# A graph, attention and MLP layer on one core: target rows of the last 18 edge tiles added by their gather

## The reference

```
feat  = concat(xn[src], xn[dst])               # 8192 x 2048
e     = relu(feat @ W + b)                     # three kinds of edge, each with its own W (2048 x 1024)
logit = e @ W_a + b_a                          # one number per edge
alpha = softmax of logit over the edges with the same dst
z     = segment_sum(alpha * xn[src], dst)
new   = relu(concat(xn, z) @ W_node + b_node)
```

## Time and profile before

| engine | busy us | share of the span | instructions |
|---|---|---|---|
| TensorE (PE) | 598.5 | 94% | 2858 |
| VectorE (DVE) | 505.2 | 80% | 843 |
| ScalarE (ACT) | 280.6 | 44% | 467 |
| GpSimd (POOL) | 219.1 | 34% | 177 |

### The profile page before, as it was taken

How to read it: one execution, slowest core, us unless ns; L and a number is a source line. 1 busy time by engine, 2 the same in 40 slices (tenths; PEclk the granted TensorE clock), 3 DMA queues, 4 the chain that set the end, 5 groups by cost and what they waited for, 6 DMA issues and landing times.

```text
span 635.2 us, 8449 instructions
## 1 busy us (share of the span) xinstructions
PE 598.5 (94%) x2858; PEld 465.9 (73%) x2860; DVE 505.2 (80%) x843; ACT 280.6 (44%) x467; POOL 219.1 (34%) x177
## 2 busy tenths in 40 slices
PE   5999999999999999969999999999999989999845
PEld 3788888888888887758888888888886327887422
DVE  6868961659859798968969978899989996648885
ACT  3335324443435253546454445754435994412201
POOL 3000040277636747236627735255110000214320
PEclk9999999999999999979999999999999999999987
DMA  8852563699999999788979959699984213895514
GB/s 326 345 188 97 208 225 124 215 376 415 417 407 356 390 389 398 299 314 299 366 292 319 409 202 382 223 329 325 393 278 181 85 27 135 295 256 188 155 39 127
DMA packets 44910, 171.43 MB, mean 270 GB/s; under 512 B 5572, under 2 KB 5956, under 8 KB 37700
## 3 DMA queue, kind: packets, MB, share of 16 engines
q1 hardware_dynamic: 20016, 86.19, 36.3%
q0 software_dynamic: 21744, 79.90, 35.0%
q10 hardware_dynamic: 3108, 4.81, 2.5%
HBM read 154.08 MB, written 16.80 MB: 269 GB/s over the span
## 4 chain that ended last, share of the span: by engine, by line
PE 56%; DVE 14%; issue 11%; DMA 8%; ACT 7%; POOL 3%; DVEq 0%; another core or an unknown queue 0%; POOLq 0%; ACTq 0%
PE bank_low L1638 15%; PE bank_low L1640 15%; PE bank_low L1639 15%; DMA w_raw<-in_wt 4%; DMA gathered_dst<-edge_tables,dst_row 2%; ACT w_hi L710 2%; ACT hot_hi L834 2%; DVE w_lo L1012 2%; PE bank_high L1640 2%; PE bank_high L1638 1%; PE bank_high L1639 1%; DVE gathered_rows L1191 1%; PE bank_high L1870 1%; PE bank_low L1993 1%; DMA edge_tables<-stage 1%
## 5 line engine op out<-in xcount | busy, mean ns | idle before, releaser
L1638 PE MATMUL bank_low<-w_hi,xT_hi 128*128 128x512 f32 x476 | 188.5, 396 | 6.3 <-ACT bank_low L741 5.4
L1640 PE MATMUL bank_low<-w_hi,xT_lo 128*128 128x512 f32 x476 | 186.1, 391 | 0.0
L1639 PE MATMUL bank_low<-w_lo,xT_hi 128*128 128x512 f32 x476 | 186.0, 391 | 0.0
L623 POOL DMA_INDIRECT gathered_rows<-edge_tables,src_row x68 | 99.2, 1459 | 156.6 <-DVE gathered_rows L1197 112.9
L710 ACT ACTIVATE w_hi<-w_raw 128x2048 fp32r<-128x2048 f32 x49 | 93.9, 1916 | 121.9 <-DMA w_raw<-in_wt 70.5
L1012 DVE TENSOR_TENSOR w_lo<-w_raw,w_hi 128x2048 fp32r<-128x2048 f32 x49 | 112.0, 2290 | 32.9 <-ACT w_hi L710 32.4
L1638 PEld LDWEIGHTS bank_low<-w_hi,xT_hi 128*128 128x128 f32 x476 | 89.9, 189 | 25.6 <-ACT bank_low L741 5.8
L1640 PEld LDWEIGHTS bank_low<-w_hi,xT_lo 128*128 128x128 f32 x476 | 89.8, 189 | 19.1
L1639 PEld LDWEIGHTS bank_low<-w_lo,xT_hi 128*128 128x128 f32 x476 | 90.0, 189 | 18.2
L1191 DVE TENSOR_TENSOR gathered_rows<-gathered_rows,gathered_dst 128x1024 f32<-128x1024 f32 x68 | 82.9, 1219 | 10.3 <-DMA gathered_dst<-edge_tables,dst_row 6.5
L623 POOL DMA_INDIRECT gathered_dst<-edge_tables,dst_row x68 | 80.8, 1189 | 20.7 <-issue 20.7
(11 more groups left out here) (304 smaller groups left out, 882.2 us busy)
## 6 DMA issues: line engine op xcount, KB each, us to landing
w_raw<-in_wt SPq DMA_DIRECT2D x54, 1024.0 KB
edge_tables<-stage SPq DMA_DIRECT2D x32, 256.0 KB
bias_bc<-in_bias_rows ACTq DMA_DIRECT2D x16, 256.0 KB
x_in<-in_x SPq DMA_DIRECT2D x4, 512.0 KB, 9.4
xn_scratch<-xn SPq DMA_DIRECT2D x4, 512.0 KB, 6.5
node_top<-stage SPq DMA_DIRECT2D x8, 256.0 KB
mix_out<-stage SPq DMA_DIRECT2D x8, 256.0 KB
xn_raw<-xn_scratch SPq DMA_DIRECT2D x4, 512.0 KB, 7.9
```

The source lines that it names most:

```text
L623: pool.indirect_dma_start(dest, None, table_d[0:nodes, :], bass.IndirectOffsetOnAxis(ap=index[:, t:t + 1].bitcast(U32), axis=0), compute_o ...
L1638: pe.matmul(dest, lh, rh, start=start and i == 0, stop=False, skip_group_check=True)
L1639: pe.matmul(dest, lh, rl, start=False, stop=False, skip_group_check=True)
L1640: last = pe.matmul(dest, ll, rh, start=False, stop=last_one, skip_group_check=True)
```

## The change

Tiles 50 to 67 leave the list `ADDED_HERE`. So the second branch of GpSimd's loop and of `edge_tile` applies to them. GpSimd's wait before the loads of `dst_bc` is for the 50 adds that VectorE still makes.

```diff
-ADDED_HERE = list(range(T_GATHERED))
+ADDED_HERE = list(range(50))
...
         pool.wait_ge(dst_stored, 16)
-        pool.wait_ge(row_added_here, T_GATHERED)
+        pool.wait_ge(row_added_here, len(ADDED_HERE))
```

## The result

The changed kernel takes 648.55 us (median of 4 runs, 648.01 to 650.67), the kernel before 641.4 us (4 runs, 640.56 to 643.44): 1.0113 times the time, 95% interval 1.008 to 1.0146. It is slower by 7.2 us; the forecast was 7.0 (a median of 648.3).

A forecast was written before the change was run, and what follows sets the result against it. The prediction took TensorE, full from 402 to 465 us, as the bound, with DMA engines 91.7% taken. Shift 7.3 less 0.3 gives 7.0 us: 644.1 profiled, plus 4.2 to the median, 648.3; range 641.2 to 652.

The forecast's parts named there:

- Nothing to gain: Removing 18 VectorE adds, 20.5 us, gives back at most the 0.3 us TensorE wait at 401.9 us.
- The price of an accumulating gather: Each accumulating gather takes 2.74 us of all 16 DMA engines against 1.43 plain, so 1.3 us more for each of 18.
- Place 1: Tiles 50 to 53, before 402 us: loss 0.2, gain 0.3, taken as -0.3 to 0, up to +3 if adds land late.
- Place 2: Tiles 59 to 67, from 404 us: crowded DMA engines land add 64 near 456 us and add 67 at 469 us.
- (a): At PR1's h1, due 457.10 us: late add 64 makes TensorE wait some 2.4 us for `w_lo`.
- (b): At the transposes, line 1788: after add 67 the last minimum ends at 470.95 us, so TensorE waits 3 us more.
- (c): At the lookup, line 1809: `hot_T` comes late, TensorE waits 1.5 us, and the lookup ends at 477.0 us instead of 469.66.
- A: Rival, both places: each add lands before VectorE comes to it, so nothing slows: 641.1 us; chance 0.17, including 0.05 for gain.
- B: Rival, last tiles: accumulating costs no more than plain; the issue chain alone shifts the end 2.9 us: 644.0 us; chance 0.20.
- C: Rival, behind TensorE's new waits: the clock drops too, 2 to 4 us on top: 650.3 to 652.3; chance 0.18 with D.
- D: Rival, tiles 52 and 53: it also breaks at place 1, +1 to +3 us on top of 648.3; chance 0.18 with C.
- The rule of the skill: For gathers at both places: 2.0 us plus bytes over 436 GB/s, 3.2 us, no accumulating surcharge; time would not change.

The follow-up runs named there:

- accumulate_beside: Kernel before with VectorE's adds and order kept; only the target gathers of tiles 50 to 67, into their own buffer, accumulate: 649.71 us, ratio 1.016.
- only_50_58: Kernel before with target rows of tiles 50 to 58 alone added by their gather, 59 to 67 by VectorE: 641.46 us, ratio 1.0011.
- only_65_67: Kernel before with target rows of tiles 65 to 67 alone added by their gather: 646.25 us, ratio 1.0109.
- plain_65_67: Kernel before with tiles 65 to 67 in the new gather order, but plain second gathers overwriting the source rows, sum left out: 641.75 us, ratio 1.0046.
- only_59_67: Kernel before with target rows of tiles 59 to 67 alone added by their gather: 650.18 us, ratio 1.0139.
- plain_second: Changed kernel, same issues, order and waits, but second gathers of tiles 50 to 67 plain, overwriting source rows, sum left out: 641.39 us, ratio 1.0009 to before.
- control: The kernel before, unchanged, run and profiled once more: 642.16 us, ratio 1.0016; profiled execution 641.18 us.
- tiles_26_28: Kernel before with target rows of tiles 26, 27 and 28 alone added by their gather: 645.08 us, ratio 1.0062.
- lag_1: Changed kernel with the target gather issued one turn after the source gather instead of two: 647.0 us, ratio 1.0161 to the kernel before.
- held_65_67: Kernel before with only tiles 65 to 67 added by gather and the three dst_bc loads held back until dot 67: 649.67 us, ratio 1.0168.

## Why the prediction was right

- **Nothing to gain (at most 0.3 us):** right. The wait at 401.9 is gone, and of the 20.5 us saved on VectorE 19.3 come back as waiting at line 1197. That VectorE's adds are worth nothing there follows from the waits of TensorE, not from VectorE's 60.99 of 63 us.
- **The price of an accumulating gather (2.74 us of 16 engines, from the earlier trace rows):** right. accumulate_beside gives 2.83 at the same bytes; in the kernel after q0 takes 64.2% of 404 to 470 us, 42.4 us, for nine plain and eleven accumulating ones: (42.4 - 12.9) / 11 = 2.68. The rows for it came from other tensors, and that didn't matter: the packets took 327 or 328 ns there too.
- **Place 1 (tiles 50 to 53, -0.3 to 0):** right. The adds of tiles 52 and 53 were issued at 374.63 and 378.43; VectorE waited 1.6 and 2.0 us for them, TensorE had no wait at line 1888, and only_50_58 bears out nine tiles in all. The prediction let the landing take 7 us; from issue to dot it was 6.5 and 10.3. In only_50_58 tile 52 waited 3.0 us, and TensorE 0.9 at a `w_lo`: the margin is thin.
- **Place 2, landing of adds 64 and 67 (456 and 469):** the dots started at 455.66 and 469.87, in an execution that was 1.3 us ahead at the first L1888 (378.45 against 379.78), so 1 to 2 us later than forecast when counted from there. The mechanism was right: the landing of add 67 sets everything behind it. The working that gave its time is weaker than the number. It summed all DMA work from 404 us on, 70.4 us, as if every microsecond of it were in the way of add 67. By that sum, half the surcharge should cost about half and three adds (3.9 us more against 4.8 free) nothing. only_65_67 costs 1.09%, 7 us, and 50 to 58 cost nothing that can be told. The pace of the dots explains the second half: a tile needs 1.43 + 2.83 = 4.3 us of the engines, and beside the 47.2% of q1 and q10 that is 8 us of time, about the 7.7 between the dots of tiles 53 and 59, but far more than the 3.3 behind tile 59. The first half, three adds that cost nearly as much as nine, the prediction's working can't give. Free engine time in the stretch as a whole (4.8 us) was the wrong measure; what counts is the slack of the last landing, and plain_65_67 shows that there is none. Its total came out right partly by luck.
- **(a) TensorE waits 2.4 us at `w_lo`:** 2.65 us, but at another place. The waits of ScalarE in the kernel after, from 402 to 472:

```profile
ACT w_hi L710 <- DMA w_raw<-in_wt: 27.8, 4, 11.5
ACT stage L731 <- DMA mix_out<-stage: 7.7, 2, 6.8
```

  A store of the output took so long that ScalarE waited 6.76 us for its buffer, until 451.56, and seeded the next bank with the bias only at 452.25, from where TensorE starts. In only_59_67 it is `w_lo`, 1.3 us. Not only the gathers are late: over the same stretch of before ScalarE waited 17.8 us for weights, and 4.4 at most for such a store. The prediction counted the loads and stores as load on the gathers and did not ask what they do when late.
- **(b) 3 us more at line 1788:** 3.27. The slow clock behind the first wait had taken 1.5 us before; without it the wait would have been some 4.8, so the agreement of the size is partly chance.
- **(c) 1.5 us at line 1809:** there was no wait, but the 1.5 us were there. The transposes and the first matmuls behind them ran at the lower clock (0.54 over 471.90 to 475.10) and took 1.5 us longer, which filled the time in which TensorE would have waited for `hot_T`. VectorE's way from the last minimum to `hot_T`, on which the step rests, took 4.2 us, forecast 4.3.
- **Rivals.** A (hidden) is out by every run with accumulating gathers of tiles 65 to 67. B (chain alone, 644.0) is out by plain_second, 641.39, with a stretch only 0.4 us longer than `control`'s. C was half right: the clock did go, at waits of 2.65 and 3.27 us and not only at one near 5.4, but it put nothing on top, since it filled waits. D did not occur in the kernel after.
- **The sum.** It gave one shift of 7.3 us at the lookup. That shift was 8.6 against `control` and 9.2 against the execution that the sum started from. The profiled execution took 648.01, where the prediction had 644.1; the medians differ by 7.2. So the mechanism held and the size was some 1 to 2 us short; that the medians came within 0.2 us of the forecast is luck.
- **The rule of the skill.** In plain_second and in the kernel after the same bytes go in the same order, and the time differs by 7 us. The fit of the Trainium skill, page "DMA: Bandwidth & Descriptors", section "Anatomy of one DMA — SWDGE (gpsimd) path", gives both kinds of gather the same estimate, 3.2 us, so by it the two kernels would take the same time. The runs do not agree.

**Open.** The 16.7 us of the last add in only_65_67 are accounted for only by the estimate of 4.2 us of engine time at q0's share; how the engines divide their time among the queues wasn't tried. Why the profiled stretch of accumulate_beside holds only 6.0 us of a loss of about 10, and where tiles_26_28 loses 4, isn't shown. That the clock fell because of the waits is read from where it fell; no run removed the waits and kept the rest of the change.

## What to carry to other kernels

Work moved from a compute engine to a DMA is paid in the DMA engines' time: here an accumulating gather cost about twice a plain one of the same bytes, and a price taken from other tensors held within 4%. Before moving such work, look at the DMA share of the stretch in which it runs and, above all, at the slack of the last landing: where tiles were wanted every 3.3 us with a consumer right behind the last, three gathers cost some 6 or 7 us; where they were wanted every 7.7 us, nine cost nothing that could be told, at full DMA engines both times. A test with the new order but the cheap kind of transfer, beside one with the old order and the dear kind, settles in two runs whether the order or the kind is the cause. And a slow clock or a wait of TensorE is not a loss by itself: compare when the engine that it waits for was ready.

## What the runs showed of the hardware that was not expected

- An accumulating packet of 4096 bytes holds its DMA engine for 327 or 328 ns, alone or beside other traffic, a plain one for 159.
- TensorE's clock fell to its lower level, 1.2 GHz (0.50), after waits of only 2.65 and 3.27 us, with the engine full before them, and was back at 1.00 by 477 us. Each time the matmuls behind took about 1.5 us longer. It fell behind shorter waits too: in plain_second and only_50_58 it is 0.50 and 0.51 from 474.2 to 477.5, after waits of 0.9 and 1.3 us at line 1809, and neither run has a loss.
- Issuing takes longer too: in the kernel after, 1849 ns of GpSimd for an accumulating gather on the mean against 1165 for a plain target gather.
- TensorE's long wait near 278 us was 5.4 us in the profiles of before, control, only_50_58 and after, 3.6 in accumulate_beside and held_65_67, 2.7 in lag_1, in a stretch that none of these edits touches. By the first L1888 held_65_67 (377.39) and control (381.17), with the same code up to there, stand 3.8 us apart, which is why the stretches above are cut at instructions.
